# Integer weights converted by GpSimd, split by ScalarE and VectorE half a step apart, over 29 half steps of the experts' last block

## The chip, the core and the metric

The kernel runs on one core of a Trainium2 chip: TensorE for matrix products, VectorE (DVE in the profile), ScalarE (ACT), GpSimd (POOL), and SyncE (SP), whose queue issues the loads and stores. The metric is the device time of one launch in microseconds (us), the median of three runs.

## The reference, cut to what matters

A sequence of 2048 rows of 256 numbers goes through two layers. The change lies in the last stage, a feed-forward network whose weights are integers:

```python
def _qlinear(x, wq, scale):
    W = (wq.astype(jnp.float32) - ZERO_POINT) * scale[:, None]
    return jnp.einsum('bsd,hd->bsh', x, W)
gate = silu(_qlinear(x, wq_gate, s_gate))          # wq_gate, wq_up: 704 x 256 int32
up = _qlinear(x, wq_up, s_up)
return _qlinear(gate * up, wq_down, s_down)        # wq_down: 256 x 704 int32

x = x + _layernorm(attention(_layernorm(x)))
x = x + _layernorm(experts(_layernorm(x)))         # 8 routed experts and a shared one
x = x + _layernorm(recurrence(_layernorm(x)))      # alpha = exp(..), beta = sqrt(1 - alpha**2), linear scan
x = x + _layernorm(integer_ffn(_layernorm(x)))
```

## The kernel before

The first phase (to about 1250 us) is the attention. The second phase, in which the change lies, holds the experts, the recurrent layer and the integer network. It cuts the 2048 rows into four blocks of 512 (`NB` = 4, numbered 0 to 3). A **step** `s` is one block with one tile of 128 hidden units. The experts need `NFM` = 14 tiles (the last has 96 units), so steps 0 to 55 are theirs, 14 to a block; the integer network needs `NFQ` = 6, steps 56 to 79.

Each step runs `up` (12 matrix products of 512 columns into three PSUM banks `pGU` in turn, for the routed experts also one into `pW`), `gate` (silu on ScalarE into `sgb`, then the multiply into `hb` on VectorE, which for routed experts is multiplied again with `pW`), `split` (ScalarE rounds `hb` to `h_hi`, VectorE subtracts: `h_lo = hb - h_hi`), and `down` (12 products into `pY`). Every operand of a product is kept as such a pair of a rounded part and a rest, and so are the weights in `W_all`.

The order is written out as a list `plan`, made from `slots`, two per step: step `s` has `up(s + 2)` and `split(s + 1)` in slot `2s`, `down(s)` and `gate(s + 2)` in slot `2s + 1`. Each engine walks the whole plan and issues what is its own, in this order; only semaphores tie the engines. In the slots behind a block's last step lie that block's layer norms and its recurrent layer (`lru_gate`, `alpha` with the exponentials, `square`, `one_less`, `beta` with the square root, `driven`, two `scan`, two `s_turn`), beside the next block's steps: those of block 2 lie beside the steps of block 3. Within the norms VectorE measures, GpSimd makes the scale and offset of it (`pool_rsqrt`, L141 and L143, then L1556 and L1558), and ScalarE applies them.

The weights come in **pieces** of 128 x 256, loaded by SP into six buffers `raw` (`SLOTS` = 6); a load waits for the subtraction (`w_lo`) of the piece six earlier. The 18 pieces of the integer network (`k` = 0 to 17; each third one is of the down weights and is also multiplied with its scales `sdb`) are to replace the experts' tiles in `W_all`, so their rounding waits until block 3's `down` has read the tile. Floats of them stand in two buffers `fl`, used in turn. Before the change the pieces of tile `m` stand together, three in a row, in slot `2 * (NMOE - NFM + m) + 2`, that is 86, 88, ... 96:

```python
dve.tensor_scalar(fl[:, k % 2], rawi, -ZERO_POINT, None, ALU.add)      # then w_float
act.activation(all_pieces[n][1], fl[:, k % 2], ACT.Copy)               # rounded, waits w_float, then w_hi
dve.tensor_tensor(all_pieces[n][2], fl[:, k % 2], ..., ALU.subtract)   # rest, waits w_hi, then w_lo
```

Of the kernel before, what the change touches and what calls it, by code (L numbers as in the profile page):

```python
# [20 lines left out]
I32 = mybir.dt.int32  # L21
ALU = mybir.AluOpType
ACT = mybir.ActivationFunctionType
# [46 lines left out]
def f(ap):  # L70

    return ap.bitcast(F32)


def build(nc, x, w_lat, w_qn, w_qpe, w_kn, w_v, w_o, q_ln, kv_ln, cos2, sin2, gw, wg, wu, wd, sel,
          l_in, l_gate, l_b, l_lam, qg, qu, qd, sg, su, sd, out):
    with ExitStack() as whole:
# [1117 lines left out]
        with ExitStack() as banks:  # L1195
# [16 lines left out]
            def at_slot(n, *step):  # L1212
                slots[n].append(step)
# [52 lines left out]
            at_slot(3 + 3 * (N_PARTS - 1) // 2, "route_turn", 1)  # L1266
            for m in range(NFQ):
                at_slot(2 * (NMOE - NFM + m) + 2, "pieces", ("q", m))
            plan = [("pieces", 0), ("logits", 1), ("route_turn", 0), ("up", 0), ("pieces", 1), ("up", 1), ("gate", 0), ("split", 0), ("gate", 1),
# [45 lines left out]
            with nc.Block() as block:  # L1315
# [108 lines left out]
                def _(act):  # L1424
# [88 lines left out]
                    def pieces(what):  # L1513
                        count = KD if what in ("in", "gate") else 3
                        for n in range(piece_no[what], piece_no[what] + count):
                            if whole_number(n):
                                if n % 3 == piece_no[what] % 3:
                                    act.wait_ge(sem("downed"), NMOE - NFM + what[1] + 1)
                                k = n_whole(n)
                                act.wait_ge(sem("w_float"), k + 1)  # L1520
                                if len(all_pieces[n][0].shape) == 2:
                                    act.activation(all_pieces[n][1], fl[:, k % 2], ACT.Copy).then_inc(sem("w_hi"), 1)
                                else:
                                    act.activation(all_pieces[n][1], fl[:, k % 2].rearrange("p (k n) -> p k n", k=KD), ACT.Copy).then_inc(sem("w_hi"), 1)  # L1524
                            else:
                                piece_hi(act, raw, all_pieces, n)

                    def route_turn(half):
# [4 lines left out]
                    def route_(part):  # L1533
                        if part == 1:
                            less_exp(act, 0)

                    does = {"route": route_, "route_turn": route_turn, "gate": silu, "split": high, "sums": sums, "y_norm": y_norm, "x_norm": x_norm, "x_turn": x_turn,
                            "lru_gate": lru_gate, "alpha": alpha, "square": square, "beta": beta, "s_turn": s_turn, "pieces": pieces}
                    for what, a in plan:
# [4 lines left out]
                def _(pool):  # L1544
                    ch = Chain(pool, sem("pool_step"))
                    pool.memset(eps[:], 0.25e-6)
                    pool.memset(carry[:], 0.0).then_inc(sem("eps_ready"), 1)
                    for step in plan:
                        if step[0] not in ("y_measure", "x_measure"):
                            continue  # L1550
# [10 lines left out]
                def _(dve):  # L1561
# [88 lines left out]
                    def pieces(what):  # L1650
                        count = KD if what in ("in", "gate") else 3
                        for n in range(piece_no[what], piece_no[what] + count):
                            if not whole_number(n):
                                piece_lo(dve, raw, all_pieces, n)
                                continue
                            k = n_whole(n)
                            rawi = raw[:, n % SLOTS, :].bitcast(I32)
                            dve.wait_ge(sem(f"w_in{n % SLOTS}"), 16 * (n // SLOTS))
                            less = dve.tensor_scalar(fl[:, k % 2], rawi, -ZERO_POINT, None, ALU.add)  # L1659
                            if k % 3 == 2:  # L1660
                                ch.inc(less)
                                ch.wait()
                                dve.wait_ge(sem("scales_in"), 48)
                                less = dve.tensor_tensor(fl[:, k % 2], fl[:, k % 2], sdb[:], ALU.mult)
                            less.then_inc(sem("w_float"), 1)
                            dve.wait_ge(sem("w_hi"), n + 1)
                            if k % 3 == 2:
                                dve.tensor_tensor(all_pieces[n][2], fl[:, k % 2], f(all_pieces[n][1]), ALU.subtract).then_inc(sem("w_lo"), 1)
                            else:
                                dve.tensor_tensor(all_pieces[n][2], fl[:, k % 2].rearrange("p (k n) -> p k n", k=KD), f(all_pieces[n][1]),  # L1670
                                                  ALU.subtract).then_inc(sem("w_lo"), 1)

# [5 lines left out]
                    def route_(part):  # L1678
                        n = t_index["logits", 1]
                        if part == 0:  # L1680
# [3 lines left out]
                    does = {"route": route_, "route_turn": route_turn, "gate": hidden, "split": low, "y_measure": y_measure, "x_add": x_add, "x_measure": x_measure, "x_turn": x_turn,  # L1684
                            "gated_x": gated_x, "one_less": one_less, "driven": driven, "scan": scan, "pieces": pieces}
                    for what, a in plan:
# [80 lines left out]
```

## Time and profile before

| | |
|---|---|
| median of 3 runs | 1692.69 us (1691.25 to 1694.73) |
| profiled execution | 1694.81 us, of which the span is 1693.0 us |
| TensorE (PE) busy | 1569.2 us, 93% |
| its weight loads (PEld) | 1319.0 us, 78% |
| VectorE (DVE) busy | 1187.9 us, 70% |
| ScalarE (ACT) busy | 1018.2 us, 60% |
| GpSimd (POOL) busy | 306.4 us, 18% |

The shares are means over the whole span; what counts for the change is the part from 1480 us on, when the experts' last block runs. The page shows the span in 40 slices of 42.3 us. A timeline row gives the start, the duration, the engine and line, what is written from what, and in brackets how long the engine had idled and whose result ended that. A row of stages gives the stretch, its length, the busy time of each engine with the number of instructions, the granted clock of TensorE as a share of full speed, and the DMA share. A row of groups gives busy time and mean duration, then the idle time before its instructions.

### The profile page before, as it was taken

To read this page: it belongs to the slowest core of one execution; us is meant where nothing else is said; L and a number is where in the kernel's file an instruction comes from. 1 tells how busy PE (TensorE), PEld (TensorE's weight loads), DVE (VectorE), ACT (ScalarE), POOL (GpSimd) and SP (SyncE) were. 2 spreads that over 40 slices of the span, in tenths; PEclk is the share of its full clock that TensorE was granted. 3 is DMA by queue.
4 is the path that set the end of the run, shared out by engine and by line. 5 is a ranking of instruction groups with operands and counts; after the bars stand their busy time and mean duration, and the time that the engine had idled before them with its cause. 6 is when DMAs were issued, how large, how long until landed. Compare 5 with 4: busy or idle time off the path is not lost. (4 is left out here: it accounts for less than half of the span.)

```text
span 1693.0 us, 38154 instructions
## 1 busy us (share of the span) xinstructions
PE 1569.2 (93%) x14508; PEld 1319.0 (78%) x14508; DVE 1187.9 (70%) x2498; ACT 1018.2 (60%) x2008; POOL 306.4 (18%) x751
## 2 busy tenths in 40 slices
PE   5789998999999999999999999999969999989997
PEld 4577787877788788888888888888857778767886
DVE  5567777776777777787788778778637646565564
ACT  3456665765666666677677667667515455545573
POOL 5411111111111211211121221121010002020231
PEclk9899999999999999999999999999869999999999
DMA  7000000000000000000000000000002100010000
GB/s 225 19 2 1 2 2 1 2 2 2 1 2 2 1 2 2 1 2 2 2 2 2 2 2 2 2 2 2 2 22 75 49 1 1 1 32 7 1 26 26
DMA packets 27397, 22.49 MB, mean 13 GB/s; under 512 B 9532, under 2 KB 25020, under 8 KB 27092
## 3 DMA queue, kind: packets, MB, share of 16 engines
q1 hardware_dynamic: 27220, 20.05, 4.1%
q8 instruction: 121, 1.98, 0.5%
q14 instruction: 56, 0.46, 0.1%
HBM read 17.95 MB, written 2.10 MB: 12 GB/s over the span
## 5 line engine op out<-in xcount | busy, mean ns | idle before, releaser
L962 ACT ACTIVATE pT_hi<-pT 128x512 f16<-128x512 f32 (+3 forms) x640 | 341.2, 533 | 305.8 <-PE pT L871 303.1
L1085 DVE TENSOR_TENSOR pT_lo<-pT,pT_hi 128x512 f16<-128x512 f32 (+3 forms) x640 | 387.4, 607 | 152.4 <-ACT pT_hi L962 146.2
L951 ACT ACTIVATE pr<-pS,nmx 128x512 f32<-128x512 f32 (+3 forms) x640 | 400.4, 626 | 21.5 <-DVE nmx L1076 19.8
L1073 DVE TENSOR_REDUCE cmx<-pS 128x1 f32<-128x512 f32 x576 | 338.8, 616 | 62.8 <-PE pS L858 58.3
L871 PE MATMUL pT<-ident,pr 128*128 128x128 f32 x2176 | 348.2, 276 | 16.1 <-DVE pT_lo L1085 14.5
L871 PEld LDWEIGHTS pT<-ident,pr 128*128 128x128 f32 x2176 | 252.6, 140 | 54.4 <-ACT pr L951 25.9
L856 PE MATMUL pS<-lT_hi,qT_hi 128*128 128x512 f32 (+2 forms) x640 | 280.6, 438 | 4.2 <-ACT pr L951 2.7
L922 PE MATMUL pO<-c_hi,pT_hi 128*128 128x65 f16 x2176 | 266.6, 194 | 17.8 <-DVE O L1103 17.8
L923 PE MATMUL pO<-c_lo,pT_hi 128*128 128x65 f16 x2176 | 267.4, 193 | 0.0
L924 PE MATMUL pO<-c_hi,pT_lo 128*128 128x65 f16 x2176 | 264.7, 192 | 0.0
L1340 PE MATMUL pGU<-lT_hi,W_all 128*128 128x512 f32 (+1 forms) x640 | 222.3, 406 | 17.5 <-ACT sgb L1433 12.3
L858 PE MATMUL pS<-lT_hi,qT_lo 128*128 128x512 f32 (+2 forms) x640 | 235.1, 367 | 0.0
L857 PE MATMUL pS<-lT_lo,qT_hi 128*128 128x512 f32 (+2 forms) x640 | 234.7, 367 | 0.0
L922 PEld LDWEIGHTS pO<-c_hi,pT_hi 128*128 128x128 f16 x2176 | 206.5, 97 | 28.3 <-ACT pT_hi L962 21.1
L923 PEld LDWEIGHTS pO<-c_lo,pT_hi 128*128 128x128 f16 x2176 | 204.7, 98 | 6.7
L924 PEld LDWEIGHTS pO<-c_hi,pT_lo 128*128 128x128 f16 x2176 | 205.9, 97 | 0.0
L1340 PEld LDWEIGHTS pGU<-lT_hi,W_all 128*128 128x128 f32 (+1 forms) x640 | 121.9, 190 | 50.0 <-ACT sgb L1433 16.7
L1030 POOL TENSOR_TENSOR qt<-qs,sn 128x128 f32<-128x128 f32 x64 | 29.2, 456 | 682.1 <-ACT qs L939 682.1
L858 PEld LDWEIGHTS pS<-lT_hi,qT_lo 128*128 128x128 f32 x640 | 120.5, 188 | 19.5
L141 POOL TENSOR_SCALAR rs<-mv 128x2 f32<-128x2 f32 (+1 forms) x72 | 18.9, 262 | 642.9 <-DVE mv L1596 365.5
L856 PEld LDWEIGHTS pS<-lT_hi,qT_hi 128*128 128x128 f32 x640 | 123.3, 193 | 9.1 <-ACT qT_hi L943 1.9
L1340 PE MATMUL pGU<-lT_lo,W_all 128*128 128x512 f32 (+1 forms) x320 | 129.0, 403 | 0.0
(277 smaller groups left out, 2606.2 us busy)
## 6 DMA issues: line engine op xcount, KB each, us to landing
X<-in_x SPq DMA_DIRECT2D x4, 512.0 KB, 7.5
wo<-in_w_o SPq DMA_DIRECT2D x1, 2048.0 KB, 10.2
out<-X SPq DMA_DIRECT2D x8, 256.0 KB, 2.0
raw<-in_wd SPq DMA_DIRECT2D x14, 128.0 KB, 2.5
raw<-in_wg SPq DMA_DIRECT2D x13, 128.0 KB, 2.5
raw<-in_wu SPq DMA_DIRECT2D x13, 128.0 KB, 2.8
wqn<-in_w_qn SPq DMA_DIRECT2D x1, 1536.0 KB, 15.4
raw<-in_qg SPq DMA_DIRECT2D x6, 128.0 KB, 2.5
```

Source lines behind the costliest of these rows:

```text
L856: pe.matmul(o, q_hi, lT_hi[:, 2, ks], start=not diagonal, stop=False, skip_group_check=diagonal)
L857: pe.matmul(o, q_hi, lT_lo[:, 2, ks], start=False, stop=False, skip_group_check=diagonal)
L858: pe.matmul(o, q_lo, lT_hi[:, 2, ks], start=False, stop=True, skip_group_check=diagonal).then_inc(sem("scored"), 1)
L871: m = pe.transpose(o[:, k * P:(k + 1) * P], pr[:, at % RING, k * P:(k + 1) * P], ident[:])
L922: pe.matmul(o, hi, c_hi[:, j, 0:KVL + 1], start=(j == 0), stop=False)
L923: pe.matmul(o, hi, c_lo[:, j, 0:KVL + 1], start=False, stop=False)
L924: m = pe.matmul(o, lo, c_hi[:, j, 0:KVL + 1], start=False, stop=(j == tile_at(p)))
L951: act.activation(pr[:, at % RING, 0:n * P], pS[at % 4][:, 0:n * P], ACT.Exp, bias=nmx[:, p % 4:p % 4 + 1]).then_inc(sem("exped"), 1)
L962: act.activation(pT_hi[:, a % 4, 0:chunk[a][2] * P], src, ACT.Copy).then_inc(sem("t_hi"), 1)
L1073: ch.inc(dve.tensor_reduce(cmx[:, p % 2, c:c + 1], pS[at % 4][:, 0:n * P], AX.X, ALU.max))
L1085: dve.tensor_tensor(pT_lo[:, a % 4, 0:w], src, pT_hi[:, a % 4, 0:w], ALU.subtract).then_inc(sem("t_lo"), 1)
L1340: mm = pe.matmul(pGU[bank % 3][0:r, :], W_all[:, m, 2 * g + i, k * P:k * P + r], xT[j][:, k, ts], start=(q == 0), stop=(q == 5))
```

## The change

GpSimd makes the floats of the integer pieces (new function `whole_float`), VectorE no longer does. The rounding on ScalarE (`whole_hi`) and the subtraction on VectorE (`whole_lo`) become plan steps of their own, `("low", k)`, one slot behind `("float", k)`. Piece `k` has its float in slot `86 + 8 * k // 5` and its split in the slot behind it, so that 18 pieces spread over slots 86 to 114 instead of three in a row in six slots. A `("pieces", ("q", m))` step stays, which numbers the pieces but issues nothing on ScalarE and VectorE.

```diff
-            for m in range(NFQ):
-                at_slot(2 * (NMOE - NFM + m) + 2, "pieces", ("q", m))
+            Q0 = 2 * (NMOE - NFM) + 2
+            for k in range(3 * NFQ):
+                if k % 3 == 0:
+                    at_slot(Q0 + 8 * k // 5, "pieces", ("q", k // 3))
+                at_slot(Q0 + 8 * k // 5, "float", k)
+                at_slot(Q0 + 8 * k // 5 + 1, "low", k)
...
+                    def whole_hi(k):
+                        n = piece_no["q", 0] + k
+                        if k % 3 == 0:
+                            act.wait_ge(sem("downed"), NMOE - NFM + k // 3 + 1)
+                        act.wait_ge(sem("w_float"), k + 1)
...
+                    def whole_float(k):
+                        n = piece_no["q", 0] + k
+                        pool.wait_ge(sem(f"w_in{n % SLOTS}"), 16 * (n // SLOTS))
+                        if k >= 2:
+                            pool.wait_ge(sem("w_lo"), n - 1)
+                        less = pool.tensor_scalar(fl[:, k % 2], raw[:, n % SLOTS, :].bitcast(I32), -ZERO_POINT, None, ALU.add)
+                        if k % 3 == 2:
+                            ch.inc(less)
+                            ch.wait()
+                            pool.wait_ge(sem("scales_in"), 48)
+                            less = pool.tensor_tensor(fl[:, k % 2], fl[:, k % 2], sdb[:], ALU.mult)
+                        less.then_inc(sem("w_float"), 1)
...
-                            dve.wait_ge(sem(f"w_in{n % SLOTS}"), 16 * (n // SLOTS))
-                            less = dve.tensor_scalar(fl[:, k % 2], rawi, -ZERO_POINT, None, ALU.add)
...
+                    def whole_lo(k):
+                        n = piece_no["q", 0] + k
+                        dve.wait_ge(sem("w_hi"), n + 1)
+                        if k % 3 == 2:
+                            dve.tensor_tensor(all_pieces[n][2], fl[:, k % 2], f(all_pieces[n][1]), ALU.subtract).then_inc(sem("w_lo"), 1)
```

VectorE in slots 86 to 88, before: the first three pieces stand between `lT_lo` (the split of a transposed norm) and the multiplies of step 45.

```order
L1624 TENSOR_TENSOR lT_lo<-pT_2,lT_hi 128x2x256
L1659 TENSOR_SCALAR fl<-raw 128x256
L1670 TENSOR_TENSOR W_all<-fl,W_all 128x256
L1659 TENSOR_SCALAR fl<-raw 128x256
L1670 TENSOR_TENSOR W_all<-fl,W_all 128x256
L1659 TENSOR_SCALAR fl<-raw 128x256
L1664 TENSOR_TENSOR fl<-fl,sdb 128x256
L1668 TENSOR_TENSOR W_all<-fl,W_all 128x256
L1578 TENSOR_TENSOR hb<-pGU_1,sgb 128x512
L1582 TENSOR_TENSOR hb<-pW,hb 128x512
L1624 TENSOR_TENSOR lT_lo<-pT_2,lT_hi 128x2x256
```

The same place after the change (L1599, L1603 are the multiplies, L1610 is `h_lo`, L1632 the addition to `X`, L1683 the subtraction of a piece).

```order
L1645 TENSOR_TENSOR lT_lo<-pT_2,lT_hi 128x2x256
L1599 TENSOR_TENSOR hb<-pGU_1,sgb 128x512
L1603 TENSOR_TENSOR hb<-pW,hb 128x512
L1645 TENSOR_TENSOR lT_lo<-pT_2,lT_hi 128x2x256
L1632 TENSOR_TENSOR X<-X,y 128x512
L1683 TENSOR_TENSOR W_all<-fl,W_all 128x256
L1610 TENSOR_TENSOR h_lo<-hb,h_hi 128x512
L1632 TENSOR_TENSOR X<-X,y 128x512
L1614 BN_STATS stats<-X 128x6 x2
L1616 BN_AGGR mv<-stats 128x2
L1617 BN_AGGR mv<-stats 128x2
L1683 TENSOR_TENSOR W_all<-fl,W_all 128x256
```

The conversions and the multiplication with `sdb` are gone from the engine, and one piece's subtraction stands in slots 87 and 88 each, behind the step's multiplies.

ScalarE in slots 98 to 103, before: the exponentials of block 2's recurrent layer (L1494), the squares (L1498) and the square root (L1502), each with its table load, between the silus (L1433) and `h_hi` (L1443).

```order
L1443 ACTIVATE h_hi<-hb 128x512
L1494 ACT_TABLE_LOAD
L1494 ACTIVATE was_keys_hi<-was_keys_hi,z 128x512 x2
L1433 ACT_TABLE_LOAD
L1433 ACTIVATE sgb<-pGU_1 128x512
L1498 ACTIVATE was_keys_lo<-was_keys_hi 128x1024
L1443 ACTIVATE h_hi<-hb 128x512
L1433 ACTIVATE sgb<-pGU_1 128x512
L1502 ACT_TABLE_LOAD
L1502 ACTIVATE was_keys_lo<-was_keys_lo,eps 128x1024
L1443 ACTIVATE h_hi<-hb 128x512
```

After the change (L1498 now the exponentials, L1502 the squares, L1506 the square root, L1437 silu, L1447 `h_hi`, L1531 and L1529 the rounding of a piece):

```order
L1498 ACT_TABLE_LOAD
L1498 ACTIVATE was_keys_hi<-was_keys_hi,z 128x512 x2
L1531 ACTIVATE W_all<-fl 128x256
L1437 ACT_TABLE_LOAD
L1437 ACTIVATE sgb<-pGU_1 128x512
L1502 ACTIVATE was_keys_lo<-was_keys_hi 128x1024
L1529 ACTIVATE W_all<-fl 128x256
L1447 ACTIVATE h_hi<-hb 128x512
L1437 ACTIVATE sgb<-pGU_1 128x512
L1506 ACT_TABLE_LOAD
L1506 ACTIVATE was_keys_lo<-was_keys_lo,eps 128x1024
L1531 ACTIVATE W_all<-fl 128x256
```

The roundings of pieces 7, 8 and 9 now stand behind the exponentials, behind the squares and behind the square root.

VectorE in slots 100 to 104, before: `h_lo` (L1589), `one_less` (L1633), the multiplies (L1578, L1582), `driven` (L1638) and the two scans (L1645).

```order
L1589 TENSOR_TENSOR h_lo<-hb,h_hi 128x512
L1633 TENSOR_SCALAR was_keys_lo<-was_keys_lo 128x1024
L1578 TENSOR_TENSOR hb<-pGU_1,sgb 128x512
L1582 TENSOR_TENSOR hb<-pW,hb 128x512
L1589 TENSOR_TENSOR h_lo<-hb,h_hi 128x512
L1638 TENSOR_TENSOR was_keys_lo<-was_keys_lo,was_keys_hi 128x1024
L1578 TENSOR_TENSOR hb<-pGU_1,sgb 128x512
L1645 SCALAR_TENSOR_TENSOR was_keys_lo<-was_keys_hi,carry,was_keys_lo 128x512
L1589 TENSOR_TENSOR h_lo<-hb,h_hi 128x512
L1645 SCALAR_TENSOR_TENSOR was_keys_lo<-was_keys_hi,carry,was_keys_lo 128x512
```

After the change (L1610 `h_lo`, L1654 `one_less`, L1599 and L1603 the multiplies, L1659 `driven`, L1666 the scans, L1683 a piece's subtraction):

```order
L1610 TENSOR_TENSOR h_lo<-hb,h_hi 128x512
L1654 TENSOR_SCALAR was_keys_lo<-was_keys_lo 128x1024
L1599 TENSOR_TENSOR hb<-pGU_1,sgb 128x512
L1603 TENSOR_TENSOR hb<-pW,hb 128x512
L1683 TENSOR_TENSOR W_all<-fl,W_all 128x256
L1610 TENSOR_TENSOR h_lo<-hb,h_hi 128x512
L1659 TENSOR_TENSOR was_keys_lo<-was_keys_lo,was_keys_hi 128x1024
L1599 TENSOR_TENSOR hb<-pGU_1,sgb 128x512
L1666 SCALAR_TENSOR_TENSOR was_keys_lo<-was_keys_hi,carry,was_keys_lo 128x512
L1683 TENSOR_TENSOR W_all<-fl,W_all 128x256
L1610 TENSOR_TENSOR h_lo<-hb,h_hi 128x512
L1666 SCALAR_TENSOR_TENSOR was_keys_lo<-was_keys_hi,carry,was_keys_lo 128x512
```

The subtractions of pieces 9 and 10 now stand in front of an `h_lo`, the second of them between the two scans.

## Rows read from the trace of the kernel before

**Rows 1.** The page's slices: busy tenths of TensorE, and its granted clock.
```profile
PE   5789998999999999999999999999969999989997
...
PEclk9899999999999999999999999999869999999999
```

**Rows 2.** Stages: us, busy us (count) of PE, PEld, DVE, ACT, POOL; clock; DMA.
```profile
1406.84:1476.68 69.84, 69.63 (x383) 55.58 (x383) 41.60 (x79) 38.38 (x62) 10.66 (x30) 1.00 0.00 1
1479.86:1566.42 86.56, 75.64 (x383) 57.74 (x383) 55.59 (x121) 45.52 (x80) 10.81 (x30) 0.94 0.07 19
1284.00:1356.00 72.00, 72.00 (x396) 57.10 (x396) 51.73 (x116) 33.15 (x72) 4.34 (x12) 1.00 0.22 62
```

**Rows 3.** Timeline of VectorE, the multiply of three steps: start, us, what.
```profile
1476.68 0.69 DVE L1578 TENSOR_TENSOR hb<-pGU,sgb 96x512 f32<-96x512 f32 x1 [1.54 <-ACT sgb L1433]
...
1479.86 0.69 DVE L1578 TENSOR_TENSOR hb<-pGU,sgb 128x512 f32<-128x512 f32 x1 [0.97 <-PE pGU L1340]
...
1566.42 0.69 DVE L1578 TENSOR_TENSOR hb<-pGU,sgb 96x512 f32<-96x512 f32 x1 [1.54 <-ACT sgb L1433]
```

**Rows 4.** Waits in block 3: total us, times, longest.
```profile
PE pGU L1340 <- ACT sgb L1433: 10.8, 5, 2.6
DVE W_all L1670 <- ACT W_all L1524: 9.7, 12, 3.1
ACT W_all L1522 <- DVE fl L1664: 6.9, 6, 1.2
...
ACT W_all L1524 <- DVE fl L1659: 5.3, 8, 1.0
```

**Rows 5.** Groups by form, 1494 to 1550: count, busy us, mean ns, idle before.
```profile
L1659 DVE TENSOR_SCALAR fl<-raw 128x256 f32<-128x256 int32 x18 | 5.1, 284 | 0.0
L1670 DVE TENSOR_TENSOR W_all<-fl,W_all 128x256 fp32r<-128x256 f32 x12 | 5.1, 425 | 9.7 <-ACT W_all L1524 9.7
L1524 ACT ACTIVATE W_all<-fl 128x256 fp32r<-128x256 f32 x12 | 5.0, 416 | 8.3 <-DVE fl L1659 5.3 <-PE pY L1359 3.0
...
L1664 DVE TENSOR_TENSOR fl<-fl,sdb 128x256 f32<-128x256 f32 x6 | 2.6, 425 | 0.2
```

**Rows 6.** Groups by form of GpSimd, whole span.
```profile
L1031 POOL TENSOR_TENSOR qt<-qs,sn 128x128 f32<-128x128 f32 x64 | 29.2, 457 | 0.0
...
L495 POOL TENSOR_TENSOR wk<-wk,kln 128x1024 f32<-128x1024 f32 x1 | 2.4, 2361 | 0.0
...
L488 POOL CAST c_hi<-latn 128x128 f16<-128x128 f32 x8 | 2.3, 289 | 0.0
...
L514 POOL CAST selb<-raw 24x1408 bf16<-24x1408 f32 x1 | 1.3, 1346 | 0.0
```

**Rows 7.** Timeline of block 2 at the recurrent layer: ScalarE, TensorE, VectorE.
```profile
1456.14 1.52 ACT L1494 ACTIVATE was_keys_hi<-was_keys_hi,z 128x512 f32<-128x512 f32 x2
...
1461.50 0.38 PE L1347 MATMUL pW<-wT,selb 24*128 24x512 bf16 x1 [0.21 <-DVE hb L1582]
...
1463.91 1.15 ACT L1502 ACTIVATE was_keys_lo<-was_keys_lo,eps 128x1024 f32<-128x1024 f32 x1
...
1465.62 0.69 DVE L1589 TENSOR_TENSOR h_lo<-hb,h_hi 128x512 fp32r<-128x512 f32 x1 [0.79 <-ACT h_hi L1443]
...
1469.91 1.28 DVE L1645 TENSOR_TENSOR_SCAN was_keys_lo<-was_keys_hi,carry,was_keys_lo 128x512 f32<-128x512 f32 x1
...
1471.72 0.60 PE L1405 MATMUL pT<-ident,was_keys_lo 128*128 128x128 f32 x4
```

**Rows 8.** Timeline, GpSimd's norm chain beside VectorE's h_lo.
```profile
1489.79 0.19 POOL L141 TENSOR_SCALAR rs<-mv 128x2 f32<-128x2 f32 x1 [0.67 <-DVE mv L1596]
...
1491.13 0.22 POOL L1558 TENSOR_SCALAR nmr<-nmr 128x2 f32<-128x2 f32 x1
...
1491.98 0.66 DVE L1589 TENSOR_TENSOR h_lo<-hb,h_hi 128x512 fp32r<-128x512 f32 x1
...
1492.14 0.54 POOL L141 TENSOR_SCALAR rs<-mv 128x2 f32<-128x2 f32 x1 [0.79 <-DVE mv L1596]
```

More of the change, by code:

```diff
@@ L1515, in pieces @@
                         for n in range(piece_no[what], piece_no[what] + count):
[L1516 to L1525, printed above, removed]
-                                piece_hi(act, raw, all_pieces, n)
+                            if not whole_number(n):
+                                piece_hi(act, raw, all_pieces, n)
+                    def whole_hi(k):
[4 more added lines that the diff above has]
+                        if k % 3 == 2:
+                            act.activation(all_pieces[n][1], fl[:, k % 2], ACT.Copy).then_inc(sem("w_hi"), 1)
+                        else:
+                            act.activation(all_pieces[n][1], fl[:, k % 2].rearrange("p (k n) -> p k n", k=KD), ACT.Copy).then_inc(sem("w_hi"), 1)
                     def route_turn(half):
@@ L1537, in _ @@
                     does = {"route": route_, "route_turn": route_turn, "gate": silu, "split": high, "sums": sums, "y_norm": y_norm, "x_norm": x_norm, "x_turn": x_turn,
-                            "lru_gate": lru_gate, "alpha": alpha, "square": square, "beta": beta, "s_turn": s_turn, "pieces": pieces}
+                            "lru_gate": lru_gate, "alpha": alpha, "square": square, "beta": beta, "s_turn": s_turn, "pieces": pieces,
+                            "low": whole_hi}
                     for what, a in plan:
@@ L1547, in _ @@
                     pool.memset(carry[:], 0.0).then_inc(sem("eps_ready"), 1)
+                    def whole_float(k):
[10 more added lines that the diff above has]
+                        less.then_inc(sem("w_float"), 1)
                     for step in plan:
+                        if step[0] == "float":
+                            whole_float(step[1])
                         if step[0] not in ("y_measure", "x_measure"):
@@ L1654, in pieces @@
                                 piece_lo(dve, raw, all_pieces, n)
-                                continue
-                            k = n_whole(n)
-                            rawi = raw[:, n % SLOTS, :].bitcast(I32)
-                            dve.wait_ge(sem(f"w_in{n % SLOTS}"), 16 * (n // SLOTS))
-                            less = dve.tensor_scalar(fl[:, k % 2], rawi, -ZERO_POINT, None, ALU.add)
[L1660 to L1671, printed above, removed]
+                    def whole_lo(k):
+                        n = piece_no["q", 0] + k
+                        dve.wait_ge(sem("w_hi"), n + 1)
+                        if k % 3 == 2:
+                            dve.tensor_tensor(all_pieces[n][2], fl[:, k % 2], f(all_pieces[n][1]), ALU.subtract).then_inc(sem("w_lo"), 1)
+                        else:
+                            dve.tensor_tensor(all_pieces[n][2], fl[:, k % 2].rearrange("p (k n) -> p k n", k=KD), f(all_pieces[n][1]),
+                                              ALU.subtract).then_inc(sem("w_lo"), 1)
                     def route_turn(half):
@@ L1684, in _ @@
                     does = {"route": route_, "route_turn": route_turn, "gate": hidden, "split": low, "y_measure": y_measure, "x_add": x_add, "x_measure": x_measure, "x_turn": x_turn,
-                            "gated_x": gated_x, "one_less": one_less, "driven": driven, "scan": scan, "pieces": pieces}
+                            "gated_x": gated_x, "one_less": one_less, "driven": driven, "scan": scan, "pieces": pieces, "low": whole_lo}
                     for what, a in plan:
```

## The prediction, made before the result was known

> **What bounds the kernel now.** I read the page's slices first. TensorE is busy in nine tenths or more of nearly every slice; counted from 1, the digits below 9 behind the start are slice 7, slice 30 (where the second phase begins, with a lower clock), slice 36 and the last one [rows 1]. Slice 36 is 1481 to 1524 us, and the change is made there. More telling is the comparison by stages. The second phase works through the experts in four blocks of 14 steps. A step's multiply on VectorE (hb<-pGU,sgb) is a good clock, since the last step of a block is the one with 96 rows: block 2 ends at 1476.68, block 3 begins at 1479.86 and ends at 1566.42 [rows 3]. Both blocks hold the same TensorE work, and beside it the same recurrent-layer work for the block before. Block 2's first multiply starts at 1406.84, so from the first multiply to the last one block 2 takes 69.84 us and block 3 takes 86.56 us [rows 2]: **16.72 us more for the same matrix products**. In block 2 TensorE is busy 69.63 of 69.84 us at a clock of 1.00; in block 3 it is busy 75.64 of 86.56 us at 0.94 [rows 2]. So block 2 is bound by TensorE and block 3 by something else.
>
> The list of waits names it. In block 3 TensorE waits 10.8 us, five times, for ScalarE's silu output. ScalarE in turn waits 6.9 us and 5.3 us for the floats that VectorE makes of the integer weights, and VectorE waits 9.7 us for ScalarE's rounded half of them [rows 4]. That is the ping-pong of the 18 integer pieces: three pieces in a row, six times, float on VectorE, rounding on ScalarE, subtraction on VectorE, each engine standing in program order behind the other, while that step's silu waits behind them on ScalarE. The rest of the 16.72 us is TensorE at a lower clock after its pauses and at a lower rate (0.94 against 1.00) [rows 2].
>
> **What the change removes.** The three-in-a-row pattern goes. If nothing took its place, block 3 would run as block 2 does: **-16.72 us**. Can the pieces be had for nothing at all? In the first block, from 1284 to 1356, three pieces per step (float weights, so rounding and subtraction only) are split beside the matrix products, and TensorE is busy in all 72.00 us at clock 1.00 [rows 2]. There are 1.3 pieces per step here. Their load is 18 roundings of 0.416 us, 7.5 us on ScalarE, and 18 subtractions of 0.425 us, 7.7 us on VectorE [rows 5]. Added to block 2's load (ScalarE 38.38 of 69.84, VectorE 41.60) this gives at most 45.9 and 49.3 us [rows 2]: neither engine becomes the bound on the average. What counts is the order at the few places without slack.
>
> **What it adds on ScalarE.** Around the recurrent layer's exponentials ScalarE sets the pace: in block 2, exp (1456.14, 1.52 us) is followed by the table load for silu, and TensorE's pW product at 1461.50 waits 0.21 us for the multiply behind that silu [rows 7]. The margin there is nothing. The change puts piece 7's rounding exactly between the exp and the table load. **+0.42 us.** Piece 8's rounding stands behind the squares, where ScalarE afterwards waits for VectorE; hidden by that wait, and worth another 0.42 if that cover is gone.
>
> **What it adds on VectorE.** The next tight chain is one_less, driven, scan, scan, then TensorE's transposes of the states. In block 2 the second scan ends at 1469.91 + 1.28 = 1471.19 and the transpose starts at 1471.72: a margin of 0.53 [rows 7]. The change puts piece 9's rounding behind the square root, which ends at 1463.91 + 1.15 = 1465.06; rounding and subtraction follow, 0.42 + 0.43, to 1465.9, and h_hi goes the same 0.42 later, so that h_lo starts near 1466.15 where it started at 1465.62 [rows 5, 7]: +0.5. Piece 10's subtraction stands between the two scans: +0.43. Together 0.95, less the margin of 0.53: **+0.4 us** of TensorE waiting. Piece 11's subtraction is behind the second scan and delays the next multiply only, which has a half step of slack. The seven pieces before this stretch and the six behind it lie where no row of block 2 shows TensorE waiting (its idle time in the whole block is 0.21 us), so I cost them at nothing; the cover is the dozen matrix products that separate a silu from the product that needs its bank, and each piece is worth up to 0.42 us if that cover is short.
>
> **What moves to GpSimd.** VectorE loses 18 conversions of 0.284 us and 6 multiplications of 0.425 us [rows 5], 7.7 us in all. No row shows GpSimd converting int32. Its one-input rows are 128x128 in 0.289 us and 24x1408 in 1.346 us, a slope of 0.83 ns per column: 0.40 us at 256 columns. Its two-input rows are 0.457 us at 128 columns and 2.361 us at 1024, 2.1 ns per column: 0.73 us at 256 [rows 6]. Bounds for the conversion are VectorE's 0.28 below and the two-input 0.73 above; I take 0.40, the nearest kind. Sum: 18 x 0.40 + 6 x 0.73 = 11.6 us on an engine that is busy 10.66 of 69.84 us [rows 2]. It also runs ahead: float k waits only for the subtraction of k-2 and for a load that was issued six pieces earlier. So nothing is paid, unless a float stands behind a normalization on GpSimd (pieces 2, 16 and 17), which is a rival below. SP's queue is untouched, and its loads start as the subtractions free a slot; they now come spread over the block.
>
> **Sum.** -16.72 + 0.42 + 0.4 = **-15.9 us**. The profiled execution took 1694.81 us (span 1693.0 and 1.81 around it), so its like would take 1678.9. The median of the runs shown is 1692.69, 2.12 below the profiled one, so I forecast **1676.8 us**. Downstream of block 3 nothing changes: its code is the same and each stage starts 16 us earlier.
>
> **A rule weighed against the trace.** GpSimd's small scale operation takes 0.19 us at 1489.79, but 0.54 us at 1492.14, and it ends with VectorE's h_lo, which reads two SBUF tiles and runs from 1491.98 to 1492.64 [rows 8]. So the two engines do hold each other up. The Trainium skill, "SBUF — State Buffer", in its account of the shared port pair, says that a VectorE instruction with two SBUF inputs and a GpSimd instruction that reads SBUF exclude each other for the whole instruction, whichever starts first. The row agrees for GpSimd as the loser; no row here shows VectorE as the loser. By that rule every subtraction could also wait for a float, which is the second rival: 1679.1 by the rule, 1676.8 by the row, in which only GpSimd waits.
>
> **Rivals.**
> 1. *The likeliest*, as summed: block 3 near 70.7 us. Chance 0.62; its own range is 1674.5 to 1679.
> 2. *GpSimd holds VectorE up.* GpSimd's long instructions now run through the dense stretch 1462 to 1471 of VectorE. Floats 9, 10, 11 and 12 fall there; if VectorE is held for each in full, 4 x 0.40 + 0.73 = 2.3 us come on top of a chain whose margin is used up: 1679.1. For it speaks the 0.54 us row, against it that a hold needs a meeting at the wrong moment and that rows with VectorE as the loser are missing. Chance 0.15.
> 3. *Floats come late behind the norms.* Piece 2's float stands on GpSimd behind a norm chain, which takes 1.56 us (1489.79 to 1491.35 [rows 8]), and needs 0.40 + 0.73 itself: 2.7 us from the end of VectorE's measurement. ScalarE has other work for part of that time and then holds the next silu; so too at pieces 16 and 17. Three holds of 2.7 us are 8.1 us; if TensorE's lead covers half of them, +4: 1680.8. For it speaks the order, against it that in block 2 ScalarE waits for the same chain without a pause of TensorE. Chance 0.13.
> 4. *Slower than before: GpSimd's conversion is slow.* With two float buffers in turn, the pieces can't pass faster than GpSimd makes them. Blocks give 69.84 / 28 = 2.49 us per half step, 1.6 half steps per piece: 4.0 us. Above a mean of 4.0 us per piece GpSimd is the bound; from (86.56 + 3.4) / 18 = 5.0 us per piece the kernel is slower than before; at 6 us block 3 takes 108 us and the kernel 1714 us. It would need ten times the slope of [rows 6]. Chance 0.04.
> 5. *The change doesn't do what it says*: the stall comes back elsewhere in block 3, because the pieces' roundings wait in program order for something new, and the time stays within 3 us of 1692.7. Chance 0.06.
>
> **Range and chances.** What a measurement of this kernel can tell from no change is about 0.2%, 3.4 us. With nothing added the sum is 1676.0, and the runs shown spread by some 2 us to either side; rival 3 gives 1680.8. I take 1673.8 to 1681.5. Faster by over 0.2%: cases 1 to 3, and part of 5, 0.92; within 0.2%: 0.04; slower: 0.04.
>
> **What would show it.** The distance of block 3's first and last 96-row multiply should be near 70.7 us, TensorE's wait for silu in it under 2 us, clock 1.00, ScalarE's wait for floats near zero. A gap before pW in step 52 near 0.6 us shows the first added term, a gap before the transposes of the states the second. Subtractions longer than 0.43 us, or gaps ahead of them, speak for rival 2; ScalarE idle before the rounding of pieces 2, 16, 17 for rival 3; GpSimd rows above 4 us for rival 4. Wrong altogether would be: block 3 still above 80 us.

## The result, and the profile after

The changed kernel takes 1684.48 us (median of 4 runs, 1683.67 to 1685.32) against 1693.63 us of the kernel before in the same series. The ratio is 0.9948, with a 95% interval from 0.9932 to 0.9965: faster by 0.5%, some 9 us, where 15.9 us were forecast. The measured time lies 7.7 us above the forecast and above its range. The profiled execution took 1683.67 us, its span 1681.7.

The page's slices, as in [rows 1]:

```profile
PE   5789998998999899999999999999969999999997
...
PEclk9899999999999999999999999999968999999999
```

The page hardly tells the two kernels apart: in slice 36 the 8 of before has become a 9, and a gap of 2 us is a twentieth of a slice. The stages tell more. This view has the columns of [rows 2]; the stretches are block 2, block 3 (first multiply to last), four microseconds inside it, and the first six steps of the integer network.

```profile
1405.42:1475.23 69.81, 69.61 (x383) 55.54 (x383) 41.62 (x79) 38.40 (x62) 10.70 (x30) 1.00 0.00 1
1478.39:1552.68 74.29, 71.92 (x384) 56.77 (x384) 46.66 (x93) 42.13 (x75) 27.03 (x48) 0.98 0.08 22
1508.00:1512.00 4.00, 4.00 (x13) 2.67 (x14) 2.35 (x4) 1.95 (x5) 2.43 (x3) 0.59 0.24 72
1556.09:1586.51 30.42, 28.13 (x168) 24.08 (x167) 19.76 (x48) 18.83 (x36) 14.19 (x31) 1.00 0.00 1
```

Block 2 is what it was, 69.81 us. Block 3 has fallen from 86.56 us to 74.29, and not to 70.7: TensorE is idle for 74.29 - 71.92 = 2.37 us, and it is busy 2.3 us longer than in block 2 for the same products. Inside it stands a stretch with a granted clock of 0.59. The first six integer steps take 30.42 us with 2.29 us of idle; the same six took 28.14 us in the kernel before (1569.60 to 1597.74), with TensorE busy throughout. So the account of the profiles is -16.72 + 2.16 (idle beyond block 2's 0.21) + 2.29 (longer products) + 2.28 = -10.0 us, and another 1.5 us of the spans' difference of 11.3 lies ahead of block 3, where no code changed: in the profiles of this study block 3 begins anywhere from 1476.3 to 1481.9 us. That is why I compare stages.

The waits of the changed kernel from block 3's start to 1575 us, as in [rows 4]:

```profile
ACT W_all L1529 <- POOL fl L1564: 5.2, 3, 3.0
...
PE pGU L1344 <- ACT sgb L1437: 4.5, 4, 1.9
...
ACT W_all L1531 <- POOL fl L1559: 3.6, 3, 1.8
```

ScalarE still waits for floats, 5.2 and 3.6 us, but now for GpSimd, in six places and not in fourteen (pieces 2 and 13 to 17); TensorE waits 4.5 us for silu instead of 10.8. The groups by form, as in [rows 5]:

```profile
L1559 POOL TENSOR_SCALAR fl<-raw 128x256 f32<-128x256 int32 x18 | 16.9, 943 | 26.7 <-DVE W_all L1683 18.4 <-DVE W_all L1681 8.4
...
L1683 DVE TENSOR_TENSOR W_all<-fl,W_all 128x256 fp32r<-128x256 f32 x12 | 5.0, 416 | 8.9 <-ACT W_all L1531 8.9
L1531 ACT ACTIVATE W_all<-fl 128x256 fp32r<-128x256 f32 x12 | 4.9, 410 | 3.6 <-POOL fl L1559 3.6
L1564 POOL TENSOR_TENSOR fl<-fl,sdb 128x256 f32<-128x256 f32 x6 | 4.8, 806 | 0.5
```

Rounding and subtraction cost what they cost before. GpSimd's conversion takes 0.86 us (median; the mean of 0.94 holds a few longer ones) and its multiplication some 0.73 to 0.81. I had taken 0.40 and 0.73. Where this hurts shows in the timeline of the three engines around step 47's silu:

```profile
1503.38 0.54 POOL L141 TENSOR_SCALAR rs<-mv 128x2 f32<-128x2 f32 x1 [0.95 <-DVE mv L1617]
...
1504.00 0.72 POOL L143 TENSOR_TENSOR rs<-rs,mhalf 128x2 f32<-128x2 f32 x1
...
1504.80 0.20 POOL L1577 TENSOR_TENSOR nmr<-mv,rs 128x2 f32<-128x2 f32 x1
...
1505.08 0.23 POOL L1579 TENSOR_SCALAR nmr<-nmr 128x2 f32<-128x2 f32 x1
1505.27 0.86 POOL L1559 TENSOR_SCALAR fl<-raw 128x256 f32<-128x256 int32 x1
...
1506.21 0.72 POOL L1564 TENSOR_TENSOR fl<-fl,sdb 128x256 f32<-128x256 f32 x1
...
1506.97 0.42 ACT L1529 ACTIVATE W_all<-fl 128x256 fp32r<-128x256 f32 x1 [2.96 <-POOL fl L1564]
1507.29 0.58 ACT L1437 ACTIVATE sgb<-pGU 128x512 f32<-128x512 f32 x1
...
1507.92 0.50 PE L1344 MATMUL pGU<-lT_hi,W_all 128*128 128x512 f32 x1 [1.93 <-ACT sgb L1437]
```

GpSimd has the norm's chain first (1503.38 to 1505.31), then the conversion and the multiplication of piece 2, to 1506.93. ScalarE stands idle for 2.96 us at piece 2's rounding, with silu L1437 queued behind it, and TensorE waits 1.93 us for that silu. The other places where TensorE waits, with GpSimd and VectorE in the dense stretch between them:

```profile
1535.21 0.50 PE L1344 MATMUL pGU<-lT_hi,W_all 128*128 128x512 f32 x1 [0.24 <-ACT sgb L1437]
...
1541.22 1.34 POOL L1559 TENSOR_SCALAR fl<-raw 128x256 f32<-128x256 int32 x1 [3.20 <-DVE W_all L1683]
...
1541.77 1.42 DVE L1659 TENSOR_TENSOR was_keys_lo<-was_keys_lo,was_keys_hi 128x1024 f32<-128x1024 f32 x1
...
1542.64 1.15 POOL L1564 TENSOR_TENSOR fl<-fl,sdb 128x256 f32<-128x256 f32 x1
...
1545.82 1.41 DVE L1666 TENSOR_TENSOR_SCAN was_keys_lo<-was_keys_hi,carry,was_keys_lo 128x512 f32<-128x512 f32 x1
...
1547.38 0.63 PE L1409 MATMUL pT<-ident,was_keys_lo 128*128 128x128 f32 x4 [0.20 <-DVE was_keys_lo L1666]
...
1567.85 0.50 PE L1344 MATMUL pGU<-lT_hi,W_all 128*128 128x512 f32 x1 [1.23 <-ACT sgb L1437]
...
1574.25 0.50 PE L1344 MATMUL pGU<-lT_hi,W_all 128*128 128x512 f32 x1 [1.06 <-ACT sgb L1437]
```

The gaps of 1.23 and 1.06 us are the same pattern at pieces 16 and 17, each behind a norm chain on GpSimd. The two places at which I had put the added terms, the silu behind the exponentials (1535.21) and the transposes behind the scans (1547.38), cost 0.24 and 0.20 us of waiting.

### The profile page after: what moved, and what is told of

Read it like the earlier page. It is cut to its first block and busy times, and to the rows that moved or that the text cites. A ratio compares the mean times of both kernels' runs of the same rounds, so it can differ in the third digit from the quotient of the medians.

```text
span 1681.7 us, 38170 instructions
## 1 busy us (share of the span) xinstructions
PE 1564.4 (93%) x14508; PEld 1315.5 (78%) x14508; DVE 1181.7 (70%) x2474; ACT 1017.8 (61%) x2008; POOL 329.6 (20%) x775
```

## The experiments

The theory after the result, A: the floats of pieces 2, 16 and 17 stand on GpSimd behind norm chains and come late. ScalarE holds the silus behind them, and TensorE pauses. The rival, B: the work of the pieces, or GpSimd and VectorE holding each other up, costs this wherever the floats are made. All ratios are to the kernel before as measured in the same series, with 95% intervals. There are four series, in which the kernel before took 1693.63 us (the change), 1693.72 (runs 1 to 4), 1692.70 (runs 5 to 8) and 1693.29 (runs 9 to 11), so medians of different series compare to within about a microsecond only.

| kernel | median us | ratio | interval | block 3, us |
|---|---|---|---|---|
| the change | 1684.48 | 0.9948 | 0.9932 to 0.9965 | 74.29 |
| 1: four floats ahead of the norms | 1678.20 | 0.9910 | 0.9895 to 0.9925 | 70.54 |
| 2: floats in place, early | 1678.37 | 0.9909 | 0.9895 to 0.9924 | 70.37 |
| 3: floats by VectorE, spread | 1677.91 | 0.9908 | 0.9891 to 0.9925 | 71.13 |
| 4: no pieces at all | 1676.21 | 0.9899 | 0.9885 to 0.9914 | 69.57 |
| 5: only piece 2 ahead | 1681.61 | 0.9935 | 0.9921 to 0.9950 | 70.56 |
| 6: only the tail ahead | 1681.38 | 0.9934 | 0.9922 to 0.9945 | 72.74 |
| 7: float view | 1683.49 | 0.9946 | 0.9933 to 0.9958 | 74.26 |
| 8: grouped, floats by GpSimd | 1697.23 | 1.0032 | 1.0020 to 1.0044 | 90.39 |
| 9: half conversions | 1680.15 | 0.9918 | 0.9902 to 0.9934 | 72.27 |
| 10: no floats | 1678.69 | 0.9906 | 0.9889 to 0.9923 | 70.37 |
| 11: straight from the integers | 1677.95 | 0.9905 | 0.9887 to 0.9923 | 71.09 |

**1. Four floats moved ahead of the norm chains.**

```diff
-                at_slot(Q0 + 8 * k // 5, "float", k)
+                early = {2: 88, 15: 109, 16: 110, 17: 112}
+                if k in early:
+                    slots[early[k]].insert(0, ("float", k))
+                else:
+                    at_slot(Q0 + 8 * k // 5, "float", k)
```

> Only the order on GpSimd changes: the floats of pieces 2, 15, 16 and 17 are made in front of the layer norms' steps on GpSimd (half steps 88, 109, 110, 112) instead of behind them. Theory A (the floats of pieces 2, 16 and 17 come late because they stand behind norm chains, and ScalarE holds the silus behind them): TensorE's three gaps of 1.93, 1.23 and 1.06 us and the 2.3 us of lower clock behind the first one go, block 3 (first to last multiply) takes about 70.5 us instead of 74.29, ScalarE's waits for floats fall below 1 us, and the kernel gains 5 to 6.5 us on the change, some 15 us on the kernel before (ratio 0.991). Rival B (the work of the pieces itself, and GpSimd and VectorE holding each other up, costs the time wherever the floats are made): nothing or under 1 us, ratio 0.995.

1678.20 us, 6.3 us less than the change, at the places that A gave. Block 3 in this kernel, first to last multiply, and its first six integer steps:

```profile
1478.58:1549.12 70.54, 70.07 (x385) 55.81 (x385) 46.86 (x93) 42.11 (x75) 27.77 (x48) 1.00 0.08 23
1552.53:1580.08 27.55, 27.55 (x168) 24.21 (x167) 19.70 (x47) 18.83 (x36) 14.87 (x31) 1.00 0.00 1
```

And piece 2, on GpSimd (L1563, L1568) and ScalarE (the rounding L1533, the silu L1441):

```profile
1498.84 1.15 POOL L1563 TENSOR_SCALAR fl<-raw 128x256 f32<-128x256 int32 x1 [4.40 <-DVE W_all L1687]
...
1500.08 0.74 POOL L1568 TENSOR_TENSOR fl<-fl,sdb 128x256 f32<-128x256 f32 x1
...
1504.29 0.40 ACT L1533 ACTIVATE W_all<-fl 128x256 fp32r<-128x256 f32 x1
...
1504.60 0.58 ACT L1441 ACTIVATE sgb<-pGU 128x512 f32<-128x512 f32 x1
```

The float is ready at 1500.82, 3.5 us before its rounding, and the silu follows at once; ScalarE waits for no float here. What is left are waits for the floats of pieces 13 and 14, 0.92 and 0.55 us (more than the 1 us in all that was expected), which make TensorE wait for nothing. The same instructions on the same engines, with only their order on GpSimd changed: B falls.

**2. Floats in place in the load buffers, three half steps earlier.** The operations on ScalarE and VectorE read the float in `raw` instead of `fl`.

```diff
-                        if k >= 2:
-                            pool.wait_ge(sem("w_lo"), n - 1)
-                        less = pool.tensor_scalar(fl[:, k % 2], raw[:, n % SLOTS, :].bitcast(I32), -ZERO_POINT, None, ALU.add)
+                        less = pool.tensor_scalar(raw[:, n % SLOTS, :], raw[:, n % SLOTS, :].bitcast(I32), -ZERO_POINT, None, ALU.add)
...
-                at_slot(Q0 + 8 * k // 5, "float", k)
+                at = slots[max(Q0 + 8 * k // 5 - 3, 84)]
+                at.insert(sum(step[0] == "float" for step in at), ("float", k))
```

> The floats are made by GpSimd in place in the load buffers, so they wait for the load alone and not for a subtraction, and they stand three half steps earlier in the order, in front of the norms' steps. Theory A: no float is ever late, block 3 takes 70 to 70.7 us, ratio about 0.9905 to 0.991, as the run with only four floats moved or up to 0.5 us better. Rival B: as many GpSimd instructions of 0.86 and 0.73 us beside VectorE as in the change, so ratio 0.995.

1678.37 us and 70.37 us for block 3: as expected of A. All 18 floats early are worth no more than the four.

**3. Spread as in the change, floats by VectorE.** `whole_float` runs on VectorE in its half step, and GpSimd has only its norms.

> The pieces are spread as in the change, but VectorE makes the floats (0.284 us, and 0.425 us for the multiplication) one half step ahead of the split; GpSimd has only its norms. Theory A: no float stands behind a norm chain, so the late floats go, and what is paid is 7.7 us more on VectorE, hidden but for the chain between the two scans, where up to two floats (0.3 and 0.7 us) come in front of the transposes: block 3 at 70.5 to 71.5 us, ratio 0.991 to 0.992. Rival C (GpSimd was needed to unload VectorE): VectorE becomes late, ratio 0.995 or worse.

```profile
1478.10:1549.23 71.13, 70.18 (x385) 55.90 (x385) 50.46 (x111) 42.54 (x75) 11.10 (x30) 1.00 0.08 23
```

VectorE is busy 50.46 of 71.13 us and the kernel takes 1677.91 us. Only the margin in front of the transposes is used up further: TensorE waits 0.71 us there, where it waits 0.23 in run 1. C falls: VectorE had no need of GpSimd's help once the pieces were spread.

**4. No pieces.** Neither floats nor rounding nor subtraction, and 12 of 18 loads left out, so the last network works with other weights.

> Leaves out all work on the integer weights (no floats, no rounding, no subtraction, 12 of their 18 loads not made; the last network multiplies by what the experts left). The floor of the whole matter: block 3 should take block 2's 69.84 us and the kernel 16.7 us less than before, 1676.9, ratio 0.990. If it stays clearly above that (over 1679), block 3 has a cost that the pieces don't explain and the comparison with block 2 was wrong.

```profile
1478.16:1547.73 69.57, 69.57 (x383) 55.59 (x383) 41.62 (x80) 38.40 (x62) 10.70 (x30) 1.00 0.00 1
```

TensorE is busy in all of 69.57 us, and the kernel takes 17.5 us less than the one before. Block 3 takes 17.0 us less than in the kernel before. This is the floor, and it shows that the comparison of block 3 with block 2 was sound.

**5 and 6. The two parts of the first run, alone:** `early = {2: 88}`, and `early = {15: 109, 16: 110, 17: 112}`.

> Only piece 2's float is moved in front of the norms' steps on GpSimd. Theory A1 (this one late float costs the 1.93 us gap of TensorE in block 3 and the slower clock behind it, 2.3 us of longer matrix products): block 3 falls from 74.29 to about 70.5 us, the first integer steps stay as in the change (30.4 us from the first to the seventh multiply), and the kernel takes about 1680.5 us, ratio 0.9925. Rival A2 (the clock falls for a reason of its own): only 1.9 us come back, block 3 at 72.5 us.

> Only the floats of pieces 15, 16 and 17 are moved in front of the norms' steps. Theory A1: block 3 stays at 74.3 us with its gap and its lower clock, the first integer steps fall from 30.4 to about 28 us, and the kernel takes about 1682.2 us, ratio 0.9935. Together with the run of piece 2 alone the two gains should add up to that of both moved (6.5 us on the change).

The medians are 1681.61 (1678.50 to 1684.44) and 1681.38 us. Against the change's median, of another series, they fall by 2.9 and 3.1 us, 6.0 together, as against 6.3 for both moved. Against run 7, which was measured beside them and whose block 3 is that of the change, they fall by 1.9 and 2.1, only 4.0 together. So the medians don't show that the two gains add up; the stages of the profiles show it better. With piece 2 moved block 3 is

```profile
1478.77:1549.33 70.56, 70.12 (x384) 55.89 (x384) 46.85 (x93) 42.13 (x75) 27.85 (x48) 1.00 0.08 23
```

70.56 us at clock 1.00, and the six integer steps still take 30.41 us: A1's numbers for the stages, though the median came out 1.1 us above its 1680.5. With the tail moved, the six integer steps fall to 27.57 us, and the gap at piece 2 stays:

```profile
1509.87 0.50 PE L1348 MATMUL pGU<-lT_hi,W_all 128*128 128x512 f32 x1 [1.93 <-ACT sgb L1441]
```

but the clock behind it does not fall in this profile (block 3, then the four microseconds behind the gap):

```profile
1480.34:1553.08 72.74, 70.38 (x385) 55.77 (x385) 46.59 (x93) 42.22 (x75) 27.05 (x48) 1.00 0.08 23
1510.00:1514.00 4.00, 4.00 (x27) 3.23 (x28) 2.69 (x5) 3.26 (x7) 2.40 (x3) 1.00 0.24 70
```

Block 3 takes 72.74 us, where A1 gave 74.3 and the change takes 74.29, and TensorE is busy in 70.38 of it instead of 71.92. So about 1.5 us of block 3's excess comes with the lower clock behind the gap, and not every execution has it: the profiles of the change and of run 7 show it (0.59 and 0.57 from 1508 to 1512), that of run 6 doesn't, and that of run 9 doesn't behind a gap of 1.60 us. The stages add up: 74.29 - 70.56 = 3.7 us with piece 2 moved and 30.42 - 27.57 = 2.9 us with the tail moved, 6.6 together, as in run 1 (74.29 - 70.54 and 30.42 - 27.55). A2 finds no support, since block 3 with the gap gone never had a lower clock; A1 is wrong in that the gap does not always bring it.

**7. Float input for the conversion.** The load buffer is read as floats, so that nothing is converted.

> The change with the integers read as floating-point bit patterns, so that GpSimd's operation has a float input and converts nothing; the weights are then wrong numbers. Theory D (the 0.86 us of a float on GpSimd is the price of converting int32, and half of each late float's cost is that price): the operation falls to about 0.40 us, the three gaps shrink by some 0.45 us each and the kernel gains 1.5 to 2.5 us on the change. Rival E (0.86 us is what this operation costs on GpSimd with any 128x256 input): 0.86 us as before, no gain.

The median of the operation is 0.860 us against 0.859 with int32, the gaps are 1.91, 1.25 and 1.06 us. Rival E: the price is that of the operation, not of the int32 input.

**8. Grouped as before, floats by GpSimd.** All three pieces of a tile have their float and split in slot `Q0 + 2 * (k // 3)`.

> GpSimd makes the floats as in the change, but the pieces stand three in a row in six half steps as before: the move to GpSimd alone, without the spreading. Theory F (the spreading is what pays, since the ping-pong of three pieces stays): a group takes about 3.4 us of waiting and working instead of 3.9, the kernel is 0 to 4 us faster than before, ratio 0.998 to 1.000. Rival G (unloading VectorE is what pays): most of the change's 9 us, ratio 0.995.

1697.23 us, slower than the kernel before by 0.3%. Both guesses were too good. Its block 3, and the waits in it:

```profile
1481.60:1571.99 90.39, 77.26 (x383) 59.03 (x383) 49.12 (x97) 44.85 (x80) 30.34 (x54) 0.92 0.06 18
```

```profile
PE pGU L1344 <- ACT sgb L1437: 12.5, 7, 4.6
ACT W_all L1529 <- POOL fl L1564: 11.6, 6, 2.3
DVE W_all L1683 <- ACT W_all L1531: 11.1, 7, 3.1
```

The ping-pong is there in full, ScalarE waits 11.6 us for GpSimd and VectorE 11.1 us for ScalarE in these rows, and GpSimd needs 0.86 us where VectorE needs 0.28. The spreading is what pays in the change; the move to GpSimd by itself costs 3.8 us of block 3 (90.39 against 86.56) in the grouped order, and 6.6 us of the time in the spread one (the change against run 3).

**9. Half of each conversion.** 128 of 256 columns are converted.

> The change, in its own order, with GpSimd's conversion done on 128 of the 256 columns only (the rest of each float buffer holds a constant, so the weights are wrong). It takes the conversion from 0.86 us towards the 0.40 us that I had predicted. Theory H (the order is the cause, the length of the conversion adds only its own difference): each of the three late floats is some 0.4 us less late, TensorE's gaps fall from 1.93, 1.23 and 1.06 us to about 1.5, 0.8 and 0.6, and the kernel takes 1682.5 to 1683.5 us, 1 to 2 us less than the change. Rival I (with a conversion as short as predicted the prediction's costing at nothing would have held): the gaps go and the kernel takes about 1678.5 us.

The conversion takes 0.54 us (median), and TensorE's three gaps are

```profile
1505.54 0.50 PE L1344 MATMUL pGU<-lT_hi,W_all 128*128 128x512 f32 x1 [1.60 <-ACT sgb L1437]
...
1562.85 0.50 PE L1344 MATMUL pGU<-lT_hi,W_all 128*128 128x512 f32 x1 [0.34 <-ACT sgb L1437]
...
1568.93 0.51 PE L1344 MATMUL pGU<-lT_hi,W_all 128*128 128x512 f32 x1 [0.75 <-ACT sgb L1437]
```

1.60, 0.34 and 0.75 instead of 1.93, 1.23 and 1.06. 1680.15 us: 4.3 less than the change, between H's 1 to 2 and I's 6. In the profile block 3 takes 72.27 us, 2.0 less than in the change: 0.4 is less waiting (0.33 of it the smaller gap), and 1.6 are shorter products, with a clock that stayed at 1.00. The six integer steps take 29.48 us, 0.9 less. That places 3.0 us; the rest stays open, and where block 3 begins varies by more than that. With a conversion nearly as short as I had forecast there are still gaps of 2.7 us in all, where rival 3 gave 4: the order makes them.

**10. No floats, rounding and subtraction kept.** They read a constant, and the pieces are not loaded, so the last network works with other weights.

> The change without any floats: rounding and subtraction of all 18 pieces stand where they do in the change, but read a constant, GpSimd has only its norms, and the pieces are not loaded. It shows what ScalarE's 18 x 0.41 and VectorE's 18 x 0.42 us cost without GpSimd. By the prediction's two added terms block 3 should take 0.4 (piece 7's rounding behind the exponentials) plus 0.4 us (two subtractions ahead of the transposes) more than the 69.57 us without pieces, 70.4 us, and the kernel 0.5 to 1 us more than the 1676.2 us without pieces. If GpSimd's and VectorE's holding each other up matters, this run is clearly better than the one with the four floats moved (70.54 us); if not, equal to it.

1678.69 us, not below the run with the four floats moved. Block 3:

```profile
1481.91:1552.28 70.37, 70.08 (x385) 55.81 (x384) 46.37 (x92) 42.13 (x76) 11.06 (x30) 1.00 0.00 1
...
1541.55 1.22 DVE L1645 TENSOR_TENSOR was_keys_lo<-was_keys_lo,was_keys_hi 128x1024 f32<-128x1024 f32 x1
...
1545.57 1.28 DVE L1652 TENSOR_TENSOR_SCAN was_keys_lo<-was_keys_hi,carry,was_keys_lo 128x512 f32<-128x512 f32 x1
```

It takes 70.37 us, which is the 70.4 expected, and 0.17 us less than in run 1. GpSimd's 17 us beside VectorE (27.77 busy in run 1's block 3, 10.70 in run 4's) cost no more than that once nothing waits for them. (The loads of the pieces are gone in run 10 too, and what they cost is not shown apart.) `driven` and the second scan take 1.22 and 1.28 us here, 1.42 and 1.41 in the change and in run 1, and TensorE does not wait ahead of the transposes, though both subtractions stand in front of them. So the subtractions use up the margin there without a wait, and the 0.20 and 0.23 us of waiting in the change and in run 1 are what GpSimd's work beside VectorE adds. The median lies 2.5 us above that of the run without pieces, where 0.5 to 1 was expected; they are of different series, and the two intervals overlap.

**11. Straight from the integers.** ScalarE rounds 12 pieces from int32 with a bias of -128, VectorE subtracts and converts in one operation, and makes the floats of the other six in one.

```diff
-                            act.activation(all_pieces[n][1], fl[:, k % 2].rearrange("p (k n) -> p k n", k=KD), ACT.Copy).then_inc(sem("w_hi"), 1)
+                            act.activation(all_pieces[n][1], raw[:, n % SLOTS, :].bitcast(I32).rearrange("p (k n) -> p k n", k=KD), ACT.Identity, bias=zp[:]).then_inc(sem("w_hi"), 1)
...
+                            dve.scalar_tensor_tensor(out=all_pieces[n][2], in0=raw[:, n % SLOTS, :].bitcast(I32).rearrange("p (k n) -> p k n", k=KD), scalar=-ZERO_POINT,
+                                                     in1=f(all_pieces[n][1]), op0=ALU.add, op1=ALU.subtract).then_inc(sem("w_lo"), 1)
```

> A candidate that does the same computation with fewer operations: for the 12 pieces without column scales ScalarE rounds straight from the integers (with the bias -128) and VectorE subtracts in one operation that converts too; for the other 6 VectorE makes the float in one operation one half step ahead. No work of GpSimd. By theory A nothing waits for a float any more, so it should equal the run with VectorE's floats (1677.9 us) or better it by up to 1 us, ratio 0.990 to 0.9915. If ScalarE or VectorE is slower on an int32 input the tight places get longer: above 1679.

```profile
L1535 ACT ACTIVATE W_all<-raw,zp 128x256 fp32r<-128x256 int32 x12 | 6.0, 501 | 0.0
...
L1682 DVE SCALAR_TENSOR_TENSOR W_all<-raw,W_all 128x256 fp32r<-128x256 int32 x12 | 5.1, 424 | 7.9 <-ACT W_all L1535 7.9
...
L1671 DVE SCALAR_TENSOR_TENSOR fl<-raw,sdb 128x256 f32<-128x256 int32 x6 | 2.4, 403 | 0.0
```

VectorE's operation that also converts takes 0.424 us, about as long as the subtraction alone (0.416); ScalarE's rounding takes 0.50 instead of 0.41. 1677.95 us: as good as runs 1 to 3, with six operations of VectorE more than in the change and none of GpSimd. Runs 1, 2, 3 and 11 can't be told apart by their times. All stand some 2 us above the median of run 4, though each interval overlaps with its; in block 3 they stand 0.8 to 1.6 us above it.

## Why the prediction was wrong

**What bounds block 3, and what goes with the ping-pong: right.** -16.72 us were forecast for a block 3 without it; without any pieces block 3 is 17.0 us shorter and the kernel 17.5 us faster.

**The step that failed is "What moves to GpSimd", costed at nothing.** It had two parts. The size: I took 0.40 us for the conversion from the slope of two casts, and it is 0.86, above even the two-input 0.73 that I had given as the upper bound. The place: "it also runs ahead" holds for twelve pieces. ScalarE waits for the floats of the other six, and TensorE in turn at pieces 2, 16 and 17, whose floats stand behind norm chains. I had named exactly these in rival 3, with a chance of 0.13 and +4 us, on the ground that TensorE's lead would cover half of 8.1 us. TensorE waited 1.93 + 1.23 + 1.06 = 4.2 us there, so that price was met, but partly by luck: it was reckoned with a conversion of 0.40 us, and with one of 0.54 us (run 9) the gaps come to 2.7. The whole cost was higher: 6.3 us by the runs of the change and run 1, 6.6 by the stages of their profiles. Run 9 shows that the length made some of it, and run 1 that with another order on GpSimd the three gaps go at the full length. With those 6.3 us the sum would have read 1683.1, against 1684.48 measured; of the 1.4 us left, 0.9 are the base, since the kernel before took 1693.63 us beside the change and 1692.69 in the runs that I started from.

**The clock was missing from the rival's price.** A gap of 1.93 us brought 1.5 us of slower products with it in some executions. I had read this effect in block 3 before (0.94 against 1.00) and used it only for the gain.

**The two terms in tight places: right in sum by coincidence, wrong in place.** 0.42 + 0.4 us of waiting were forecast. With rounding and subtraction alone (run 10) block 3 takes 0.80 us more than the floor, but 0.29 of it is waiting, and 0.51 are longer products at a clock of 1.00, which the sum did not have. In the change the silu behind the exponentials starts 5.08 us after h_hi (1529.48 to 1534.56) instead of 4.78, 0.30 later and not 0.42. The wait before pW, 0.21 us in block 2, is not there, since the second multiply followed the first sooner; TensorE waits 0.24 us for the silu itself, before the next product into `pGU`. The two subtractions ahead of the transposes only use up the margin and make no wait (run 10): the 0.4 was wrong, and the 0.20 us seen there in the change belong to rival 2.

**Rival 2, GpSimd against VectorE: real and cheap.** GpSimd's conversion at 1541.22 takes 1.34 instead of 0.86 us, and VectorE's `driven` beside it 1.42 where it takes 1.22 in run 10. Runs 1 and 10 put the whole effect at 0.2 us of block 3, against the 2.3 of the rival. The Trainium skill, "SBUF — State Buffer", in its account of the shared port pair, lets the second of two such instructions wait for the whole first one. Of that row it is not so: `driven` starts in the trace 0.79 us before GpSimd's conversion ends and loses 0.20. The rule would have given up to 2.3 us.

**Rivals 4 and 5** did not happen: the longest conversion took 1.34 us, where rival 4 needed a mean of 4.0, and the time lies 8 us below 1692.7, where rival 5 kept it within 3. Slower than before, as in rival 4, is run 8, but by the grouping and with the same 0.86 us.

## What to carry to other kernels

When work is moved to an idle engine, don't ask how busy that engine is, but what stands in front of each moved instruction in its queue, and who stands behind the waiting one on the other side; an engine that is busy 20% of the time was late six times out of eighteen here, and three of these cost 6.3 of the 15.5 us that run 1 gained. Spreading the hand-overs so that no engine answers another within the same half step paid here, and the helper engine did not: alone it made the kernel slower. Price an operation on GpSimd from a row of the same kind and the same number of columns, or leave it where it is.

## What the runs showed of the hardware

GpSimd's `tensor_scalar` with one input takes 0.86 us for 128x256, with int32 as with float input, and 0.54 us for 128x128: about 2.5 ns per column, three times the slope of the casts in [rows 6], and longer than its two-input product (0.73 us). The Trainium skill, "GPSIMD Engine Reference", in the section on engine selection, calls one-input work roughly line-rate; for this operation the runs show otherwise (VectorE takes 0.284 us for the same). Reading int32 directly saves a separate conversion: ScalarE rounds 128x256 from int32 in 0.50 us and from floats in 0.41; VectorE subtracts from int32 in 0.42 us, as from floats (run 11).

After a pause of TensorE of 1.93 us in the change, and of 1.91 us in run 7, the granted clock fell to the lower of its two levels, 1.2 GHz:

```profile
1509.00:1512.00 3.00, 3.00 (x10) 1.82 (x10) 1.46 (x3) 0.95 (x3) 1.58 (x2) 0.50 0.31 90
```

It stayed at 1.00 behind the same pause in run 6. In the kernel before it fell behind three of the five pauses of 1.94 to 2.56 us in block 3 (those before 1500.09, 1524.08 and 1548.15 us) and stayed at 1.00 behind the other two (1508.81 and 1515.72). What decides between them stays open.
